# Sliding-window scores as 64-row products into two PSUM banks, one key tensor without zero halves, and the sums of squares in the norms' bank

## The reference

```
for i in range(6):
    x = attn_layer(shift_tokens(x), Wqkv[i], q_scale[i], k_scale[i], Wo[i]) + x
    x = ffn_layer(shift_tokens(x), ln_g[i], ln_b[i], W1[i], b1[i], W2[i], b2[i]) + x

attn_layer:                                  # 16 heads of 64, window 32
    q, k, v = split(x @ Wqkv)                # by heads
    q = l2norm(q) * qs ; k = l2norm(k) * ksc
    q = q*cos*scale + rotate_half(q)*sin*scale
    k = k*cos/scale + rotate_half(k)*sin/scale
    sim  = einsum('bhwie,bhwje->bhwij', q, [window before, own window] of k) * 8
    attn = softmax(where(mask, -max, sim))
    out  = einsum('bhwij,bhwje->bhwie', attn, [window before, own window] of v) @ Wo
```

## Time and profile before

| | us |
|---|---|
| median of three executions | 1903.41 |
| profiled execution, span of its instructions | 1897.4 |
| stage A, about 0 to 315 | 315 |
| steady part of stage B taken for rows, 380 to 1840 | 1460 |

### The profile page before, as it was taken

The page is one execution under the profiler, slowest core; times in us unless marked ns, Lnnn a source line. Parts: engine busy times, 40 slices in busy tenths (PEclk is TensorE's granted clock), DMA queues, the critical chain, the costliest instruction groups (busy, mean ns, idle before and its releaser), DMA issues.

```text
span 1897.4 us, 49036 instructions
## 1 busy us (share of the span) xinstructions
PE 1775.2 (94%) x19119; PEld 1213.9 (64%) x19119; DVE 1620.6 (85%) x2695; ACT 1157.9 (61%) x2003; POOL 1278.1 (67%) x1548
## 2 busy tenths in 40 slices
PE   7999998899999999999999999999999999999997
PEld 4545454466666666666666676666666766666675
DVE  5887785799889999899898989998999889989983
ACT  3565665456566656665666666655766666666665
POOL 5212124777688777787777788768877778777762
PEclk8999999899999999999999999999999999999999
DMA  2000011455545555555455555555555455555552
GB/s 77 1 6 1 7 41 45 155 176 172 176 161 186 181 170 165 178 174 183 163 173 172 170 179 172 187 166 169 181 183 173 164 173 183 170 180 166 188 164 80
DMA packets 190739, 275.62 MB, mean 145 GB/s; under 512 B 23278, under 2 KB 87340, under 8 KB 190252
## 3 DMA queue, kind: packets, MB, share of 16 engines
q1 hardware_dynamic: 189004, 270.48, 43.5%
q10 hardware_dynamic: 1504, 2.00, 0.3%
HBM read 72.11 MB, written 52.43 MB: 66 GB/s over the span
## 4 chain that ended last, share of the span: by engine, by line
PE 37%; DVE 29%; POOL 14%; issue 10%; ACT 8%; DMA 1%; ACTq 0%; POOLq 0%; DVEq 0%; SPq 0%
DVE turned L982 10%; DVE kz L1002 7%; PE psum L597 4%; PE psum L668 3%; PE psum L599 3%; PE psum L598 3%; PE psum L807 3%; PE psum L837 3%; DVE rd L1018 3%; PE psum L691 3%; PE psum L682 3%; POOL u L1425 3%; PE psum L741 2%; POOL sdiff L1414 2%; ACT hid L1291 2%
## 5 line engine op out<-in xcount | busy, mean ns | idle before, releaser
L982 DVE SCALAR_TENSOR_TENSOR turned<-psum,vecs,tabs 128x1024 f32<-128x1024 f32 x384 | 486.8, 1268 | 33.2 <-POOL u L1425 20.9
L1190 ACT ACTIVATE sq<-psum 128x512 f32<-128x512 f32 x384 | 227.8, 593 | 164.8 <-PE psum L599 164.0
L1414 POOL TENSOR_TENSOR sdiff<-sdiff,rqs 128x512 f32<-128x512 f32 x192 | 200.8, 1046 | 151.9 <-DVE sdiff L1014 151.6
L1425 POOL TENSOR_TENSOR qT<-turned,swapped 128x512 f32<-128x512 f32 x192 | 242.4, 1283 | 37.9 <-PE psum L775 36.6
L1425 POOL TENSOR_TENSOR u<-turned,swapped 128x512 f32<-128x512 f32 x192 | 241.5, 1279 | 37.2 <-DMA swapped<-turned 36.8
L1002 DVE TENSOR_TENSOR kz<-u,psum 64x512 f32<-64x512 f32 x384 | 255.3, 665 | 6.3 <-PE psum L763 3.7
L796 PEld LDWEIGHTS psum<-pxT,v 128*64 128x64 f32 x6144 | 194.7, 138 | 74.3 <-issue 66.7
L1396 POOL TENSOR_TENSOR px<-px,rd 128x512 f32<-128x512 f32 x192 | 201.7, 1050 | 42.2 <-DVE rd L1020 39.7
L796 PE MATMUL psum<-pxT,v 128*64 128x64 f32 x6144 | 221.2, 225 | 4.3 <-DMA pxT<-scratch 4.2
L775 PE MATMUL psum<-kz,qT 128*32 128x128 f32 x6144 | 213.4, 277 | 6.0 <-DVE kz L1002 5.8
L597 PE MATMUL psum<-xs_hi,wqk_hi 128*128 128x512 f32 x384 | 176.4, 460 | 33.8 <-DVE turned L982 30.8
(11 more groups left out here) (187 smaller groups left out, 3475.7 us busy)
## 6 DMA issues: line engine op xcount, KB each, us to landing
swapped<-turned SPq DMA_DIRECT2D x384, 256.0 KB, 2.8
scratch<-pt SPq DMA_DIRECT2D x192, 256.0 KB, 2.1
pxT<-scratch SPq DMA_DIRECT2D x384, 128.0 KB, 2.8
v<-v SPq DMA_DIRECT2D x192, 192.0 KB, 2.5
w_raw<-in_wqkv SPq DMA_DIRECT2D x36, 256.0 KB, 3.3
v<-v SPq DMA_DIRECT2D x144, 64.0 KB, 2.0
wo<-in_wo SPq DMA_DIRECT2D x12, 256.0 KB, 3.4
w_raw<-in_w SPq DMA_DIRECT2D x12, 170.5 KB, 2.5
```

What stands on the lines that cost most here:

```text
L982: engine.scalar_tensor_tensor(out=turned[:, n % NROT, :, :], in0=both, scalar=vec(("ks" if which else "qs", i)), in1=tabs[:, 2 * which:2 * ...
L1190: engine.activation(sq[:, n % NSQ, :], bank(n % 2), ACT.Square).then_inc(s_sq, 1)
L1414: engine.tensor_tensor(sdiff[:, :, :], sdiff[:, :, :], r_, ALU.mult).then_inc(s_weigh, 1)
L1425: engine.tensor_tensor(u[:, n % GT, :] if which else qT[:, m_, :], turned[:, n % NROT, 0, :], swapped[:, n % NSWAP, :], ALU.add).then_inc( ...
```

## The change

1. **Scores.** `kz` becomes `kT` (128, 8 tiles, 32 + 512), without the zero halves. Each product takes the 64 rows of one head from `qT` and `kT`, 32 columns of weights and 64 moving columns; there are 32 per unit in place of 16 of 128 rows and 128 moving columns. Even heads go to bank 3, odd ones to bank 4. Mask, maxima and difference work on both banks at once, 256 columns of each. The order of the eight heads inside `smax`, `sdiff`, `px`, `rqs` changes with it.
2. **Scale.** DVE writes a key tile in one instruction of 128 partitions, where it wrote two of 64. POOL clears only the first 32 columns of `kT`, in one instruction, not all of `kz` in eight.
3. **Sums of squares.** They no longer have a bank of their own: `square_sums` is now one step of eight products per round (`NSQ` is 8, so that all eight `sq` tiles are kept), in the ring of *norms*, *norm_rows* and *scale*, whose one bank is now bank 2.
4. **Places.** All numbers in `PLACES_A` and `PLACES` and the constants of the lists are new; two lines of them:

```diff
@@ PLACES
-    "norm_rows": dict(tensor=1.4, scalar=1.25),
+    "norm_rows": dict(tensor=1.205, scalar=1.317),
...
-    "product": dict(tensor=3.35, vector=3.5),
+    "product": dict(tensor=3.221, vector=3.745),
...
@@ build
-    kz = sb(ctx, "kz", [P, HP, 2, WIN + T])
+    kT = sb(ctx, "kT", [P, HP, WIN + T])
...
-    bank_n = ring("n", (3,))
+    bank_n = ring("n", (2,))
+    score_banks = psum[:, 3:5, 0:MU * 2 * WIN]
...
-        if step[0] in ("norms", "norm_rows", "scale"):
+        if step[0] in ("square_sums", "norms", "norm_rows", "scale"):
             bank_n.fill(*step)
...
@@ tensor
             elif kind == "square_sums":
-                pe.wait_ge(s_sq, GT * (g + 1))
-                pe.wait_ge(s_nsq, g // 2)
-                sums = pairsel[:, 0:SC] if g % 2 else pairsel[:, 2:2 + SC]
-                for j in range(GT):
-                    m = engine.matmul(bank(2)[SC * j:SC * (j + 1), :], sums, sq[:, (GT * g + j) % NSQ, :], start=g % 2 == 0,
-                                      stop=g % 2 == 1, skip_group_check=True)
-                m.then_inc(s_squares, 1)
+                pe.wait_ge(s_sq, UT * (r + 1))
+                pe.wait_ge(*bank_n.free(*step))
+                for which, sums in enumerate((pairsel[:, 2:2 + SC], pairsel[:, 0:SC])):
+                    for j in range(GT):
+                        m = engine.matmul(into[SC * j:SC * (j + 1), :], sums, sq[:, (UT * r + GT * which + j) % NSQ, :],
+                                          start=which == 0, stop=which == 1, skip_group_check=True)
+                m.then_inc(bank_n.fills(*step), 1)
...
             elif kind == "scores":
-                    for w_ in range(4):
+                    for hp, w_ in itertools.product(range(2), range(4)):
                         t0 = (4 * t + w_) * WIN
-                        m = engine.matmul(bank(4)[WIN * w_:WIN * (w_ + 1), j * P:(j + 1) * P], qT[:, m_, t0:t0 + WIN],
-                                          kz[:, m_, :, t0:t0 + 2 * WIN], start=False, stop=j == MU - 1 and w_ == 3,
-                                          skip_group_check=True)
+                        rows = slice(DH * hp, DH * (hp + 1))
+                        m = engine.matmul(score_banks[WIN * w_:WIN * (w_ + 1), hp, j * 2 * WIN:(j + 1) * 2 * WIN],
+                                          qT[rows, m_, t0:t0 + WIN], kT[rows, m_, t0:t0 + 2 * WIN], start=False,
+                                          stop=j == MU - 1 and w_ == 3, skip_group_check=True)
...
@@ vector
             elif kind == "scale":
-                for hp in range(2):
-                    s_ = slice(64 * hp, 64 * hp + 64)
-                    m = engine.tensor_tensor(kz[s_, m_, hp, WIN:], u[s_, n % GT, :], nb[s_, :], ALU.mult)
-                m.then_inc(bank_n.empties(*step), 1)
+                engine.tensor_tensor(kT[:, m_, WIN:], u[:, n % GT, :], nb, ALU.mult).then_inc(bank_n.empties(*step), 1)
             elif kind == "scores":
-                sv = bank(4).rearrange("p (k j) -> p k j", j=2 * WIN)
+                sv = score_banks.rearrange("p h (k j) -> p h k j", j=2 * WIN)
...
@@ gpsimd
             elif kind == "clear":
-                engine.memset(kz[:, m_, :, :], 0.0).then_inc(s_fill_d, 1)
+                engine.memset(kT[:, :, 0:WIN], 0.0).then_inc(s_fill_d, 1)
```

More of the change, by code:

```diff
@@ L38 @@
 WCH = INNER // 2
-NROT, NSWAP, NSQ = 4, 4, 4
+NROT, NSWAP, NSQ = 4, 4, 8
 NRQ, NXS = 4, 3
@@ L213 @@
                                                  ("w1", 1)))
[L220 to L223, removed]
+AFTER, UNIT = 33.562, 0.684
+EARLY = 10.361
+PACE, HALF = 1, 1.223
+START, UP = 7.6, 0
 PLACES = {
[L225 to L231, removed]
-    "norm_rows": dict(tensor=1.4, scalar=1.25),
[L233 to L242, removed]
-    "product": dict(tensor=3.35, vector=3.5),
[L244 to L253, removed]
@@ new lines @@
+    "shift_parts": dict(gpsimd=-0.374),
+    "heads": dict(tensor=-0.248, vector=0.502, scalar=0.052),
+    "swap": dict(sync=0.717),
+    "rotate": dict(gpsimd=1.502),
+    "square_sums": dict(tensor=0.065, scalar=0.314),
+    "norms": dict(tensor=0.55, vector=0.733, scalar=0.721),
+    "norm_parts": dict(gpsimd=0.674),
+    "norm_rows": dict(tensor=1.205, scalar=1.317),
+    "scale": dict(tensor=3.068, vector=3.394),
+    "mask": dict(scalar=-0.943),
+    "weigh": dict(gpsimd=-0.338),
+    "scores": dict(tensor=-0.366, vector=-0.098, scalar=0.302),
@@ new lines @@
+    "prob_sums": dict(vector=0.467, gpsimd=0.467),
+    "blocks": dict(vector=0.914),
+    "move": dict(sync=1.002),
+    "fetch": dict(sync=1.716),
+    "values": dict(tensor=1.099, scalar=1.327, gpsimd=1.533, sync=1.415),
+    "apply": dict(tensor=2.703, scalar=2.954),
+    "product": dict(tensor=3.221, vector=3.745),
+    "shifted": dict(scalar=3.952),
+    "token_major": dict(tensor=4.6, scalar=4.877),
+    "statistics": dict(vector=5.238, gpsimd=6.226),
+    "scaled": dict(scalar=6.691),
+    "feature_major": dict(tensor=6.781, scalar=7.238, gpsimd=7.105),
@@ L254 @@
+    "gate": dict(tensor=7.671, scalar=7.551),
+    "up": dict(tensor=8.038, vector=7.938),
+    "down": dict(tensor=9.426, vector=9.926),
+    "write_out": dict(tensor=10.742, vector=9.95, scalar=11.864, sync=12.027),
+    "blank": dict(tensor=-0.366),
 }
@@ L275, in order_b @@
     if engine == "gpsimd":
-        for m in range(HP):
-            put(0.02 * m - 0.1, "clear", m)
+        put(0.0, "clear")
     if engine == "scalar":
@@ L294, in order_b @@
         put(n / 2 + 0.5, "rotate", n + 1)
-    for g in range(NT // GT):
-        for kind in ("square_sums",) + ("norms", "norm_parts", "norm_rows") * (g % 2):
-            put(GT * (g + 1) / 2 - 0.5, kind, g)
+    for r in range(NT // UT):
+        for kind in ("square_sums", "norms", "norm_parts", "norm_rows"):
+            put(UT * (r + 1) / 2 - 0.5, kind, r)
     for n in range(NB):
@@ L516, in build @@
             bank_b.drain("act", *step)
-        if step[0] == "norm_rows":
+        if step[0] in ("square_sums", "norm_rows"):
             bank_n.drain("act", *step)
@@ L582, in query_tile, with newton @@
         return (n // TT) * UT + j
-    def newton(g):
-        return g // 2 * 5
+    def newton(r):
+        return r * 5
     def tensor(engine):
@@ L1013, in vector @@
                 dve.wait_ge(s_saved, 16 * B)
-                engine.tensor_tensor(sdiff[:, :, :], sv, mb, ALU.subtract).then_inc(s_sdiff, 1)
+                engine.tensor_tensor(sdiff[:, :, :].rearrange("p (h k) j -> p h k j", h=2), sv, mb, ALU.subtract).then_inc(s_sdiff, 1)
             elif kind == "prob_sums":
@@ L1219, in scalar @@
                 act.wait_ge(s_saved, 16 * B)
-                engine.copy(bank(4).rearrange("p (k j) -> p k j", j=2 * WIN), mask).then_inc(s_mask, 1)
+                engine.copy(score_banks.rearrange("p h (k j) -> p h k j", j=2 * WIN), mask).then_inc(s_mask, 1)
             elif kind == "scores":
```

116 lines of the change are left out of this document (57 added, 59 removed).

## The result

The changed kernel takes 1818.2 us (median of 4 runs, 1816.15 to 1820.64); the kernel before, on the same chip, 1901.7 us (1897.52 to 1903.65). The ratio is 0.9558, with a 95% interval of 0.954 to 0.9575. The profiled execution's span is 1816.1 us at a granted clock of 0.987, against 1897.4 before: 81 us less. The forecast was 1813 us, 90 us less. The total is close, but four of its terms were not, and their errors cancelled; the experiments take them one by one. The 6.0 us between span and median of the kernel before are only in part what lies around the span: wherever one execution has both numbers, its time is 1.8 to 2.1 us above its span. The rest is that the profiled execution was faster than the median.

The account below looks back on a forecast made before the run. PE was taken to bound the kernel, with DVE close behind. Scores -67, scale -22, sums of squares -6 and norm rows +5 make -90 us: span 1897.4 becomes 1807, plus 6.0 gives 1813 us, range 1777 to 1878.

Parts of the forecast that it names:

- The bound: Steady part: PE bounds, DVE close behind; PE time counts fully, DVE time only where PE waits for it, 32.5 us.
- Scores: PE's score products: both row halves run at once, 1.08 us becomes 0.73 per unit, -67 us, bounds -81 and +14.
- 64 records in 0.66 to 0.80 us: Sign in the scores' burst on PE: this duration would show the forecast for overlapping row halves right.
- taking turns: Rival on PE's scores: row halves do not overlap, about 1.15 us, +14 us, kernel at 1894 us; chance 0.10.
- the third rival: PE's scores: each record costs its start, 0.026 us, so 1.86 us per unit, kernel at 2030 us; chance 0.05.
- Scale: DVE's key tile: one instruction for two, 0.64 us less per unit; two thirds of PE's 34 us waits go, -22 us.
- near 0.69: Sign on DVE: the key instruction of 128 partitions would last near 0.69 us.
- Sums of squares: PE's square sums: one block of eight takes 1.88 us against 2.00 per round, -6 us, bounds -9 and +10.
- Norm rows: `rn` transposes on PE stand one heads step earlier and may wait: +5 us, between 0 and +34.
- The rest, at nothing: Residual sum 0, bounds -5 and +5; two-bank walks and POOL's `kz` clear 0; stage A 0, within 4 us.
- The sum: All terms together: -67 - 22 - 6 + 5 = -90 us, span 1897.4 becomes 1807, time 1813 us.
- half lost to other waits: Rival: latency chains through POOL and ACT end last, half of 90 us is gained, 1858 us; chance 0.17.

Follow-up runs that it names:

- K alone: Kernel before with only the first of two DVE key instructions per tile, second head's keys left out: 1862.0 us, ratio 0.9806.
- S alone: Changed kernel with two key instructions and the old places, leaving 64-row scores, two score banks and joined sums in the shared bank: 1919.6 us, ratio 1.0093.
- S with P: Changed kernel with the key tile written by two DVE instructions of 64 partitions again: 1896.2 us, ratio 0.9979.
- P: Kernel before with all places and constants of the changed kernel, nothing else: 1890.0 us, ratio 0.9937.
- K and P: Kernel before with one of two key instructions left out and the changed kernel's places: 1860.4 us, ratio 0.9787.
- the halves in turns: Changed kernel with score products ordered head half by head half, so the two row halves cannot run together: 1823.25 us, ratio 0.9597.

## Why the prediction came out right, and where it did not

The total was right by luck: three terms lie outside their own bounds or beyond the most that the step allowed, one (the scores) is half again too large, and the errors have opposite signs.

**The bound.** "PE is the bound and DVE is close behind", "time off PE's own work counts fully": this step failed. PE's busy time is a union of overlapping records, and a record ends long after the next could start, so short waits lie under record tails. Counted from the starts of PE's steps instead (each gap from a step's last start to the next one's first, less what the tightest tenth of such gaps takes), PE lost 119.6 of 1300 us before, 9%, where its busy time leaves 64.9; with K alone 101.7, in the changed kernel again 118.8. DVE, whose records don't overlap, was busy 1169.1 of those 1300 us: 90%, in an order in which it and PE wait for each other in turn. K alone (-37 us), with PE's work untouched, shows that DVE set the pace as much as PE did. S alone (+18) shows less: it holds the joined sums, which cost 22 by themselves. In the changed kernel no single engine does: 26 us more on PE cost 5 to 7, 96 us less on DVE gave nothing that can be measured, and two key instructions of 675 ns in place of one of 666, 0.68 x 192 = 131 us more on DVE, cost 78.

**Scores, -67 us.** The mechanism was right, the size not: 0.86 us, not 0.73. In PE's time it is 1.011 to 0.788 us from the first start to the next step's, 0.22 per unit and not 0.35: 43 us. What it is worth depends on the rest. With two key instructions S bought nothing (S with P, -4 against P's -12). As the last piece S gave 44, near the 43 and 7 of PE's time in scores and sums, so with K and P in most of it did count; yet of that, the overlap of the halves is worth only 5 to 7 us. The sign named for it, "64 records in 0.66 to 0.80 us", was missed by 0.06, and taking turns costs 0.99 us, not 1.15. Of the third rival (each record costs its start) a small part is real: the burst's last 32 records go at 13 ns apiece, under the 14 from which it decides.

**Scale, -22 us.** Mis-sized most: -37 alone and -80 as the last piece (78 between the two medians). The duration was right (666 ns against "near 0.69"), and DVE's busy time over 184 units fell by 138.8 us, 245.9 - 122.6 = 123.3 of it the key's. What failed is the price: the wait list's 34 us were taken as the most that DVE could give. A wait is booked only where PE shows idle; more of PE's lost time lies under the tails of records (119.6 us of gaps against 64.9 of idle). Which waits the 78 us came from isn't shown one by one.

**Sums of squares, -6 us.** The length was right, 1.92 and 1.86 us against 1.94 and 1.88. The price was not: +22 us alone, outside the bounds -9 and +10. The block was costed by its length and not by what stood in its old place, a wait for a key. In the changed kernel, where the key comes 0.66 us sooner, that cover is no longer needed (PE waits 1.1 us for `kT`); what the joined block costs there wasn't tried.

**Norm rows, +5 us.** Wrong in sign, by the step's choice of whose queue to look at: PE's wait for `rn` did grow, 11.8 to 16.0 us, inside the forecast's 12 to 20. ACT's queue behind the same transposes was left out, and so was PE's own wait for ACT's copy; with them the move gives 36 us, far outside the bounds 0 and +34.

**The rest, at nothing.** Stage A (4 us), the clear and the two-bank walks hold. The residual sum's "0, bounds -5 and +5" is not settled: its wait went, but the places together gave 12 to 28 us, and beyond `rn` (36 in the changed kernel, more than the 28 of all places) they weren't tried one by one. (L1009's row reads 680 ns, not the 679 of the prediction; nothing hangs on it.)

**The sum.** -67 - 22 - 6 + 5 = -90 against -84 by the ratio. In parts, added in the order K, S, P, the table reads -37, -19, -28. The rival "half lost to other waits" described PE's side better than the forecast did: in the chain that ended last POOL's share rose from 14% to 23%, and POOL's wait for the swap's DMA from 31.7 to 49.6 us (400 to 1700 us). It failed on the size, since DVE's relief paid more than its price.

## What to carry to other kernels

Where two in-order engines wait for each other by turns, don't price a change by busy shares or by the list of waits alone: the same instruction was worth 37 us alone and 80 with the others. Before moving or joining a block, ask what its old place covered, and which other engine's queue stands behind its result; for both, one run with only that block moved tells more than its length. When all parts of a change are in, run each combination at least once: here a part that loses 18 us alone was worth 44 in company.

## What the runs showed of the hardware

Products of 64 rows by 32 columns of the array, eight at once: eight starts within 0.06 us, 0.29 us for all, with starts 7 ns apart at the median inside a round. At first, rounds of eight follow each other in about 0.056 us; with the halves in turns, fours do, in (0.993 - 0.216) / 15 = 0.052: both halves together pass in the time of one. For products in different places of the array, starts came much closer than the about 25 ns of the Trainium skill, "TensorE: Matmul & The Clock Gate", section "Wait — 56ns, not 53.3ns?", that the prediction weighs. No run put both row halves into one bank, so whether the second bank is needed stays open.

In a burst of 64 such records the first 32 pass in 0.454 us, (0.454 - 0.216) / 31 = 8 ns apiece, the last 32 in the remaining 0.404, 13 ns apiece. Two bursts of 32 with other work between stay at 0.454 each. So the loss comes with the burst's length and not with its shapes. With the halves in turns the last 32 take 0.391, about as long as with both at once, and only the first 32 gain by the overlap, 0.454 against 0.602. The Trainium skill, "TensorE: Matmul & The Clock Gate", section "Architectural detail: the array is 16× 32×32, not 1× 128×128", gives TensorE a queue of 64 instructions, from which weight loads are pulled ahead of products. The runs agree with that as far as they go: 32 MATMUL rows with their 32 weight loads would be 64 instructions, if each row counts as one; the first 32 go fast and the others slower. No run varied the burst's length beyond 32 and 64 to settle it.

On DVE a product of 64x512 with a factor from PSUM took 665 ns, of 128x512 666, of 128x32 166: the columns count and the partitions don't.
